# Routed experts by scatter and gather in one stream of slots, beside dense experts in stages

## The chip, the cores and the metric

One core of a Trainium2 chip. Its engines are TensorE (PE), VectorE (DVE), ScalarE (ACT), GpSimd (POOL) and the SyncE queue (SP) that issues most DMAs. They run side by side, each works its instructions in order, and they wait for each other on semaphores. The metric is the device time of one execution in microseconds (us); the median of three runs before is 811.64 us (811.57 to 812.65).

## The reference, cut to what matters

The input x has 8 batches of 512 tokens of 128 features, all fp32. Cut to what matters:

```python
xn = layernorm(x)
# differential attention: 8 heads of 16, two maps of 8 each
scores = einsum('bqhif,bkhif->ibhqk', q, k) * 8 ** -0.5
att = softmax(scores)[0] - diff_weight * softmax(scores)[1]
o = einsum('bhqk,bkhe->bqhe', att, v)
a = (rms_norm(o) * norm_w @ Wo.T + bo) * (1 - diff_weight)
# feed forward: a shared expert and the best 2 of 8 for each token
gates = sigmoid(xn @ Wg); vals, idx = top_k(gates, 2); w = vals / vals.sum()
shared = silu(xn @ Ws1) * (xn @ Ws3) @ Ws2               # 128 -> 256 -> 128
routed = sum over experts of w[e] * (silu(xn @ We1[e]) * (xn @ We3[e]) @ We2[e])
out = x + a + (shared + routed) / 3
```

`w` is zero for six of the eight experts of every token.

## The kernel before, in words

The program goes through the batches in two alternating stages, `attend` and `ffn` (L183 on, `batches`): a hardware loop of three rounds covers two batches each, and what is first and last is written out. The order of each engine's work is written by hand; semaphores with counted values tie the engines.

Attention is computed transposed, keys on partitions. The 16 maps of a batch and four key tiles make 64 tiles of 128 keys by 512 queries. q and k are split into two fp32r parts (`qparts`, `kparts`) and laid by DMAs from SP (`lay_qk`) into operands `qop` and `kop`, in which two maps stand in the two halves of 64 partitions, so that two score matmuls of different halves can stand in the array at once. Two of the 64 rows carry the negated row maximum of a query, so that a score tile comes out with its maximum taken off. For that the maxima must be known first: `score_unit` (L840) computes the scores queries first into the banks `S`, DVE reduces two of them in one instruction of 1024 columns (`row_max`, L624), and after a batch's last one the maxima are split, transposed by PE and laid by four small DMAs (`lay_m`, L247). `score_tile` (L911) puts a tile into one of three banks `ST`, ACT takes its exponential (L474) into `probs`, a ring of 8, and four value matmuls of 32 output rows, in four column groups, add it into the bank `O` (L953). The maxima of batch b+1 are made in the attention stage of batch b: each `score_tile` is followed by a `score_unit` of the other half.

The experts are dense. All nine (eight and the shared one) run over all 512 tokens of a batch, in 18 chunks of 128 hidden features (`ffn`, L983 to L985). Each chunk is two sides of three fp32r matmuls of 512 columns (high times high, high times low, low times high, weights split once at the start and kept in SBUF as `w13h` and `w13l`), Silu on ACT (L505), the product on DVE (L748), a multiplication by the token's gate weight on POOL (L384), and one fp32 matmul down into `O` (L967), three chunks later. The gate weights come from 19 small DVE steps per batch (`top_step`), are transposed, stored to DRAM and broadcast back to all partitions. Between the chunks stand the attention's unpacking (DVE, ST banks), its projection (L1039) and the preparation of batch b+2. ACT loads its function table when it goes from exponentials to Silu and back.

## Time and profile before

| what | value |
|---|---|
| median of 3 runs | 811.64 us |
| profiled execution: time, span | 813.23 us, 811.4 us |
| PE busy | 759.4 us (94%) |
| DVE busy | 589.9 us (73%) |
| ACT busy | 428.3 us (53%) |
| POOL busy | 248.6 us (31%) |
| DMA | 45.40 MB, mean 56 GB/s |
| mean granted PE clock | 0.963 |

The span runs from the first to the last instruction. Busy times are from one profiled execution. Matmuls overlap in the array, so that PE can be shown as busy while it could take more; the starts of successive matmuls show what one costs. An fp32 matmul stands in the trace as two records, an fp32r matmul as one (its type is shown as f32 too). PEld is the loading of weights, which overlaps.

### The profile page before, as it was taken

Reading aid. Unit: us, or ns where it says so; the run is one execution under the profiler, and the core shown is the slowest. Engines: PE = TensorE matmul, PEld = TensorE weight load, DVE = VectorE, ACT = ScalarE, POOL = GpSimd, SP = SyncE. Lnnn points to the kernel's source line nnn. Section 1 sums busy time; section 2 is a strip of 40 time slices with the busy share of each in tenths; the row PEclk is TensorE's granted clock in tenths of the full one; section 3 lists DMA queues with packets and bytes.
Section 4 is the critical chain, followed back from the end, with each engine's and each line's share of the span. In section 5 each row is a group of like instructions: output and inputs, shape, how many; then the busy total and the mean of one; then the engine's idle time right before and its main releaser. Section 6 shows DMA issues by size and latency. Waiting matters only on the chain.

```text
span 811.4 us, 12753 instructions
## 1 busy us (share of the span) xinstructions
PE 759.4 (94%) x3740; PEld 406.7 (50%) x3740; DVE 589.9 (73%) x837; ACT 428.3 (53%) x799; POOL 248.6 (31%) x216
## 2 busy tenths in 40 slices
PE   4367999999999998999999998999999999999997
PEld 4122336743566335753467434663367434653464
DVE  5499998669866896659877696668986597751274
ACT  1101784268733784348832685337853587239722
POOL 5883005420155003440065101550044301530152
PEclk9665899999999999999999999999999999999999
DMA  3562101530052100511023300521015200110010
GB/s 100 133 168 80 29 1 32 130 89 4 2 144 68 40 2 21 143 52 40 2 72 88 91 2 5 135 75 43 1 28 134 72 8 2 56 52 27 1 53 13
DMA packets 36262, 45.40 MB, mean 56 GB/s; under 512 B 3736, under 2 KB 18840, under 8 KB 36184
## 3 DMA queue, kind: packets, MB, share of 16 engines
q1 hardware_dynamic: 30712, 33.70, 15.9%
q10 hardware_dynamic: 4608, 8.39, 3.6%
q0 software_dynamic: 864, 2.36, 1.1%
q8 instruction: 38, 0.62, 0.3%
q14 instruction: 40, 0.33, 0.1%
HBM read 24.78 MB, written 2.23 MB: 33 GB/s over the span
## 4 chain that ended last, share of the span: by engine, by line
PE 88%; DVE 5%; ACT 2%; issue 1%; POOL 1%; DMA 1%; SPq 1%; POOLq 0%; DVEq 0%
PE O L953 17%; PE ST L911 16%; PE O L967 16%; PE S L983 9%; PE S L985 8%; PE S L984 8%; PE S L840 5%; DVE rowmax L624 4%; PE ST L959 2%; PE ST L812 2%; PE ST L803 2%; ACT probs L474 2%; DMA kop<-kparts 1%; PE O L1039 1%; PE O L803 1%
## 5 line engine op out<-in xcount | busy, mean ns | idle before, releaser
L624 DVE TENSOR_REDUCE rowmax<-S 128x2 f32<-128x1024 f32 x256 | 307.8, 1220 | 51.2 <-PE S L840 46.4
L384 POOL TENSOR_TENSOR probs<-probs,rwb 128x512 f32<-128x512 f32 x128 | 169.1, 1323 | 523.8 <-DVE probs L748 523.8
L474 ACT ACTIVATE probs<-ST 128x512 f32<-128x512 f32 x476 | 252.3, 615 | 61.4 <-PE ST L911 58.8
L840 PE MATMUL S<-kop,qop 62*128 62x512 f32 x512 | 208.4, 507 | 26.5 <-DVE rowmax L624 14.3
L911 PE MATMUL ST<-qop,kop 64*128 64x512 f32 x476 | 177.3, 452 | 2.9 <-ACT probs L474 0.2
L748 DVE TENSOR_TENSOR probs<-S,sil 128x512 f32<-128x512 f32 x144 | 98.9, 687 | 99.5 <-PE S L985 99.0
L505 ACT ACTIVATE sil<-S 128x512 f32<-128x512 f32 x144 | 86.2, 599 | 157.9 <-PE S L985 155.2
L911 PEld LDWEIGHTS ST<-qop,kop 64*128 64x128 f32 x476 | 79.4, 187 | 151.4 <-ACT probs L474 124.6
L983 PE MATMUL S<-xh,w13h 128*128 128x512 f32 x288 | 146.5, 509 | 6.3 <-issue 6.3
L967 PE MATMUL O<-probs,w 128*128 128x512 f32 x288 | 148.0, 596 | 0.0
L953 PE MATMUL O<-probs,vop 128*32 128x512 f32 x1024 | 141.1, 608 | 0.4
L985 PE MATMUL S<-xh,w13l 128*128 128x512 f32 x288 | 114.3, 397 | 0.0
L984 PE MATMUL S<-xl,w13h 128*128 128x512 f32 x288 | 113.5, 394 | 0.0
L840 PEld LDWEIGHTS S<-kop,qop 62*128 62x128 f32 x512 | 82.9, 196 | 54.6 <-DVE rowmax L624 40.5
L983 PEld LDWEIGHTS S<-xh,w13h 128*128 128x128 f32 x288 | 54.9, 191 | 34.5 <-issue 23.8
L984 PEld LDWEIGHTS S<-xl,w13h 128*128 128x128 f32 x288 | 55.2, 192 | 21.3 <-issue 14.9
L967 PEld LDWEIGHTS O<-probs,w 128*128 128x128 f32 x288 | 53.1, 188 | 18.1 <-issue 8.0
L985 PEld LDWEIGHTS S<-xh,w13l 128*128 128x128 f32 x288 | 54.6, 190 | 12.9
L953 PEld LDWEIGHTS O<-probs,vop 128*32 128x32 f32 x1024 | 24.4, 108 | 40.4 <-ACT probs L474 25.6
L712 DVE TENSOR_SCALAR o_inv<-o_inv,ndw 128x8 f32<-128x8 f32 x32 | 34.3, 1072 | 0.9
L719 DVE TENSOR_TENSOR o_n<-o_sc 128x128 f32<-128x128 f32 x32 | 24.9, 777 | 0.8
L700 DVE COPY oT<-O 128x512 f32<-128x512 f32 x4 | 2.8, 692 | 28.2 <-PE O L953 28.2
(117 smaller groups left out, 518.0 us busy)
## 6 DMA issues: line engine op xcount, KB each, us to landing
qop<-qparts SPq DMA_DIRECT2D x32, 256.0 KB, 3.6
kop<-kparts SPq DMA_DIRECT2D x32, 256.0 KB, 6.0
rwb<-w_scr SPq DMA_DIRECT2D x32, 256.0 KB, 3.7
rwb<-w_scr ACTq DMA_DIRECT2D x32, 256.0 KB, 3.3
xin<-in_L_attn_x SPq DMA_DIRECT2D x8, 256.0 KB, 3.5
sil<-in_L_ffn_We POOLq DMA_DIRECT2D x16, 128.0 KB, 4.0
res<-in_L_attn_x SPq DMA_DIRECT2D x8, 256.0 KB, 3.2
out_x<-res SPq DMA_DIRECT2D x8, 256.0 KB, 2.3
```

What stands on the lines that cost most here:

```text
L384: nc.gpsimd.tensor_tensor(hid[:, c % NHB, :], hid[:, c % NHB, :], rwb[:, e % NRW, :], ALU.mult).then_inc(s_hw, 1)
L474: nc.scalar.activation(probs[:, s % NP, :], banks[s % len(banks)], ACT.Exp, scale=SCALE).then_inc(s_p, 1)
L505: nc.scalar.activation(sil[:, c % 2, :], S[c % 2][:, 0, :], ACT.Silu).then_inc(s_si, 1)
L624: V.reduce_max(rowmax[:, u // QT * HALVES:(u // QT + 1) * HALVES, u % QT], S[u % 2][:, :, :], AX).then_inc(s_mx, 1)
L748: V.tensor_tensor(hid[:, c % NHB, :], S[c % 2][:, 1, :], sil[:, c % 2, :], ALU.mult)\
L840: ins = mm(S[u % 2][:, h, :], qop[par][at:at + TERMS, c, t * P:(t + 1) * P], kop[par][at:at + TERMS, c, :], start=True, stop=True, tile_po ...
L911: mm(banks[s % len(banks)], kop[par][at:at + ROWS, c, t * P:(t + 1) * P], qop[par][at:at + ROWS, c, :], start=True, stop=True, tile_positi ...
L953: mm(O[VW * j:VW * (j + 1), :], vop[par][:, t, (4 * g + j) // MAPS, :], probs[:, s % NP, :], start=(t == 0), stop=(t == QT - 1), tile_posi ...
L967: mm(O[:, :], w2[:, c // FC, c % FC, :], hid[:, c % NHB, :], start=(c == 0), stop=last).then_inc(s_y, 1)
L983: mm(dst, w13h[:, c // FC, at], xh[par][:, :], start=True, stop=False)
L984: mm(dst, w13h[:, c // FC, at], xl[par][:, :], start=False, stop=False)
L985: mm(dst, w13l[:, c // FC, at], xh[par][:, :], start=False, stop=True).then_inc(s, 1)
```

## The change

The program is rewritten as one list of 146 slots, numbered -12 to 133, that every engine walks through (in the new program all loops are written out; there is no hardware loop). The 128 slots from 0 on have four score tiles each, 16 slots a batch. Slot s also computes four row maxima of slot s+12 (`LEAD`), now one bank of 512 and one DVE instruction each, and the value matmuls of slot s-1. There are two `S` banks, two `ST` banks, `O`, and three banks `F`: F[0] and F[1] for the two up sides, F[2] for down and for all side jobs of attention (`other`: transposes, projections, maxima rows). `claim` makes PE wait until a bank's last reader is done.

At the start all eight batches are normalised, transposed and gated, before the slots. 42 DVE steps (`route`), two per quarter of a slot, find each token's two experts and its two rows in a DRAM buffer `xs`, sorted by expert, each expert padded to a multiple of 256 rows. The buffer is filled with zeros by three DMAs. POOL scatters 32 tiles of 128 tokens twice by indirect DMA (64, three a slot from slot -5 on). 16 tiles of 256 tokens of the shared expert run in every second slot from -10 to 20; 39 tiles of 256 rows of routed tokens in every second slot from 24 to 100. A routed tile's weights (0.39 MB) come from DRAM by an expert number that SP reads from SBUF, asked for three slots ahead, with three buffers. Its rows are transposed on PE, both sides computed in plain fp32, silu(h) written as h * (1 + tanh(h/2)) with the half put into the weights of the sum, and its result is stored to DRAM (`ys`). From slot 103 on POOL gathers both rows of each token by indirect DMA (64, three a slot), and DVE adds them, weighted, to the output rows (`combine`, from slot 112 on). Exponentials and tanh stand mixed on ACT.

Weights are laid out on the host in the new program (transposed projections, the three matrices of an expert side by side); the split into fp32r parts is gone for the experts and stays for q and k. GpSimd also has the unpacking of attention (`unpack`, three operations per four slots). The diff is nearly the whole file; its core:

```diff
-            def ffn(b, par, more, prep):
-                pe.wait_ge(s_p, TILES * (b + 1))
-                pe.wait_ge(s_xs, 2 * b + 2)
-                pe.wait_ge(s_w13, 2 * (E + SHARED))
-                pe.wait_ge(s_wbig, 16 * (1 + FC))
-                pe.wait_ge(s_w2s, 1)
-                for c in range(CH):
-                    if more and c < 2:
-                        pe.wait_ge(s_mx, UNITS * (b + 2) - 1 + c)
-                    if c >= 2:
-                        pe.wait_ge(s_hm, CH * b + c - 1)
-                    for side, s in ((0, s_h1), (1, s_h3)):
-                        at = slice(side * FF + c % FC * P, side * FF + c % FC * P + P)
-                        dst = S[c % 2][:, side, :]
-                        mm(dst, w13h[:, c // FC, at], xh[par][:, :], start=True, stop=False)
-                        mm(dst, w13h[:, c // FC, at], xl[par][:, :], start=False, stop=False)
-                        mm(dst, w13l[:, c // FC, at], xh[par][:, :], start=False, stop=True).then_inc(s, 1)
...
+    TOK = 256
+    SH_TILES = BATCH * SEQ // TOK
+    RT_TILES = BATCH * SEQ * TOPK // TOK + E - 1
+    TILES = SH_TILES + RT_TILES
+    ROWS = RT_TILES * TOK
+    CMAX = BATCH * SEQ // TOK
+    NW = 3
+    POST = 6
+    LEAD = 12
+    SH0 = -10
+    RT0 = SH0 + 2 * SH_TILES + 2
+    GATHER0 = RT0 + 2 * RT_TILES + 1
+    COMBINE0 = SLOTS - 16
+    SCAT0 = -5
...
+            def load_tile(r):
+                if r == 0:
+                    sp.wait_ge(s_rt, R_EXP)
+                e = sp.value_load(jidx[0:1, r:r + 1], min_val=0, max_val=E - 1)
+                if r >= NW:
+                    sp.wait_ge(s_y, SH_TILES + r - NW + 1)
+                sp.dma_start(wrt[r % NW][:, :], wexp[bass.ds(e, 1), :, :].rearrange("e p f -> (e p) f")).then_inc(s_wl[r % NW], 16)
+                if r == 0:
+                    sp.wait_ge(s_sc, 16 * TOPK * NT)
+                if r >= 2:
+                    sp.wait_ge(s_xt, r - 1)
+                sp.dma_start(xst[r % 2][:, :, :], xs[TOK * r:TOK * r + TOK, :].rearrange("(p s) d -> p s d", s=2)).then_inc(s_xl[r % 2], 16)
...
+            def scatter(n):
+                i, k = n // TOPK, n % TOPK
+                if n == 0:
+                    gp.wait_ge(s_fill, 16 * (ROWS // P // 26))
+                    gp.wait_ge(s_rt, R_IDX2)
+                    gp.wait_ge(s_xn, NT)
+                G.indirect_dma_start(xs[:, :], bass.IndirectOffsetOnAxis(ap=slot_i[:, k, i:i + 1], axis=0),
+                                     xn[:, i, :], None).then_inc(s_sc, 16)
+            def gather(n):
+                b, t, k = n // (QT * TOPK), n // TOPK % QT, n % TOPK
+                if n == 0:
+                    for i in range(2):
+                        gp.wait_ge(s_yst[i], 16 * ((RT_TILES + 1 - i) // 2))
+                    gp.wait_ge(s_sc, 16 * TOPK * NT)
+                    gp.wait_ge(s_xT, BATCH)
+                if b == BATCH // 2 and t == 0 and k == 0:
+                    gp.wait_ge(s_v, BATCH)
+                G.indirect_dma_start(gbuf[b][:, k, t, :], None, ys[:, :],
+                                     bass.IndirectOffsetOnAxis(ap=slot_i[:, k, QT * b + t:QT * b + t + 1], axis=0)).then_inc(s_g[b], 16)
...
+            def tanh_half(j):
+                act.wait_ge(s_h1, j + 1)
+                if j >= 2:
+                    act.wait_ge(s_u, j - 1)
+                A(tb[j % 2][:, :, :].rearrange("p c t -> p (c t)"), F[0][:, :], ACT.Tanh, scale=0.5).then_inc(s_th, 1)
...
+                    if 0 <= slot < SLOTS:
+                        exp_tile(slot, k)
+                    if k == 0:
+                        j = tile_at(slot - 2)
+                        if j is not None and j >= SH_TILES:
+                            copy_y(j - SH_TILES)
+                        j = tile_at(slot)
+                        if j is not None and j >= SH_TILES:
+                            copy_xsT(j - SH_TILES)
+                        j = tile_at(slot - 1)
+                        if j is not None:
+                            tanh_half(j)
...
+            def row_max(slot, k):
+                n = 4 * slot + k
+                q, hf = slot % QUADS, slot // 8 % 2
+                dve.wait_ge(s_s, n + 1)
+                if slot % 8 == 0 and k == 0 and slot >= 16:
+                    dve.wait_ge(s_ms, 3 * (slot // 8 - 1))
+                V.reduce_max(rowmax[hf][:, 1 - k % 2, q // 2 % HC, (2 * q + k // 2) % QT:(2 * q + k // 2) % QT + 1],
+                             S[n % 2][:, :], AX).then_inc(s_mx, 1)
...
+            def gate_u(j):
+                dve.wait_ge(s_th, j + 1)
+                if j >= 2:
+                    dve.wait_ge(s_hid, j - 1)
+                V.scalar_tensor_tensor(out=ub[j % 2][:, :, :].rearrange("p c t -> p (c t)"),
+                                       in0=tb[j % 2][:, :, :].rearrange("p c t -> p (c t)"), scalar=1.0, in1=F[0][:, :],
+                                       op0=ALU.add, op1=ALU.mult).then_inc(s_u, 1)
+            def gate_hid(j):
+                dve.wait_ge(s_u, j + 1)
+                dve.wait_ge(s_h3, j + 1)
+                if j >= 2:
+                    dve.wait_ge(s_y, j - 1)
+                V.tensor_tensor(hid[j % 2][:, :, :].rearrange("p c t -> p (c t)"), F[1][:, :],
+                                ub[j % 2][:, :, :].rearrange("p c t -> p (c t)"), ALU.mult).then_inc(s_hid, 1)
...
+                    if slot + LEAD < SLOTS:
+                        row_max(slot + LEAD, k)
+                    for _ in range(2):
+                        if step < R_STEPS:
+                            route(step)
+                            step += 1
+                    n = (slot + LEAD) // 8 - 1
+                    if (slot + LEAD) % 8 == 0 and 0 <= n < 2 * BATCH and k < 3:
+                        max_parts(n, k)
+                    if k == 0:
+                        j = tile_at(slot - 2)
+                        if j is not None and j < SH_TILES:
+                            add_shared(j)
+                    j = tile_at(slot - 1)
+                    if j is not None and k == 1:
+                        gate_u(j)
+                    if j is not None and k == 2:
+                        gate_hid(j)
...
+            def up(j, side):
+                bank = claim(side, (s_u, s_hid)[side], j + 1)
+                if side == 0:
+                    if j == 0:
+                        pe.wait_ge(s_wsh, 16)
+                    if j < SH_TILES:
+                        pe.wait_ge(s_xTc, j // 2 + 1)
+                    else:
+                        r = j - SH_TILES
+                        pe.wait_ge(s_wl[r % NW], 16 * (r // NW + 1))
+                        pe.wait_ge(s_xtc, r + 1)
+                for c in range(FC):
+                    at = side * FF + c * P
+                    last = mm(bank[:, c * TOK:(c + 1) * TOK], weights(j)[:, at:at + P], tokens(j), start=True, stop=True)
+                last.then_inc((s_h1, s_h3)[side], 1)
+            def down(j):
+                if j < SH_TILES:
+                    bank = claim(2, s_ysh, j + 1)
                 else:
-                    pe.wait_ge(s_hw, RCH * b + c + 1)
-                mm(O[:, :], w2[:, c // FC, c % FC, :], hid[:, c % NHB, :], start=(c == 0), stop=last).then_inc(s_y, 1)
-            def ffn(b, par, more, prep):
-                pe.wait_ge(s_p, TILES * (b + 1))
-                pe.wait_ge(s_xs, 2 * b + 2)
-                pe.wait_ge(s_w13, 2 * (E + SHARED))
-                pe.wait_ge(s_wbig, 16 * (1 + FC))
-                pe.wait_ge(s_w2s, 1)
-                for c in range(CH):
-                    if more and c < 2:
-                        pe.wait_ge(s_mx, UNITS * (b + 2) - 1 + c)
-                    if c >= 2:
-                        pe.wait_ge(s_hm, CH * b + c - 1)
-                    for side, s in ((0, s_h1), (1, s_h3)):
-                        at = slice(side * FF + c % FC * P, side * FF + c % FC * P + P)
-                        dst = S[c % 2][:, side, :]
-                        mm(dst, w13h[:, c // FC, at], xh[par][:, :], start=True, stop=False)
-                        mm(dst, w13h[:, c // FC, at], xl[par][:, :], start=False, stop=False)
-                        mm(dst, w13l[:, c // FC, at], xh[par][:, :], start=False, stop=True).then_inc(s, 1)
-                    if c >= LAG:
-                        down(b, c - LAG)
-                    if more and c == 0:
-                        do_rwT(b + 1)
-                    if c == 1:
-                        pe.wait_ge(s_oe, GROUPS * (b + 1))
-                        do_oT(b, 0, 2)
-                    if more and c == 2:
-                        do_mT(b + 2, ST[1])
-                    if c == 3:
-                        if more:
-                            pe.wait_ge(s_rwc, b + 2)
-                        do_oT(b, 1, 0)
-                    if prep:
-                        x = b + 2
-                        if c == 5:
-                            pe.wait_ge(s_mc, b + 3)
-                            do_xT(x, 1)
-                        if c == 6:
-                            pe.wait_ge(s_on, OE_STEPS * b + 4)
-                            project(x, 0, 2, s_q)
-                        if c == 7:
-                            pe.wait_ge(s_on, OE_STEPS * b + 8)
-                            project(x, 1, 0, s_k)
-                        if c == 9:
-                            do_v(x, 1)
-                        if c == 11:
-                            pe.wait_ge(s_vc, x + 1)
-                            do_g(x, 1)
-                    if c == 8:
-                        pe.wait_ge(s_on, OE_STEPS * b + 4)
-                        if prep:
-                            pe.wait_ge(s_qr, b + 3)
-                        do_oT(b, 2, 2)
-                    if c == 10:
-                        pe.wait_ge(s_on, OE_STEPS * b + 8)
-                        if prep:
-                            pe.wait_ge(s_kr, b + 3)
-                        do_oT(b, 3, 0)
-                    if c == 16:
-                        pe.wait_ge(s_on, OE_STEPS * (b + 1))
-                        tiles_T(ST[2][:, :], lambda t: o_n[:, t, :], ident[:, :], s_nT)
-                for c in range(CH - LAG, CH):
-                    if more:
-                        s = c - CH + LAG
-                        if s < 2 and prep:
-                            pe.wait_ge(s_hm, CH * (b + 1) - 1)
-                        if s == 2:
-                            pe.wait_ge(s_nc, b + 1)
-                            pe.wait_ge(s_hm, CH * (b + 1))
-                        start_attend(b + 1, 1 - par, prep, True, s)
-                    if c == CH - 1:
-                        pe.wait_ge(s_nc, b + 1)
-                        mm(O[:, :], woT[:, :], nT[:, :], start=False, stop=False)
-                    down(b, c, last=c == CH - 1)
-            batches(pe, attend, ffn)
-            finish(BATCH - 1)
-_INS = ['L0_attn_x', 'L0_attn_Wq', 'L0_attn_Wk', 'L0_attn_Wv', 'L0_attn_norm_w', 'L0_attn_Wo', 'L0_attn_bo',
-        'L0_attn_diff_weight', 'L0_ffn_Wg', 'L0_ffn_Ws1', 'L0_ffn_Ws3', 'L0_ffn_Ws2', 'L0_ffn_We1', 'L0_ffn_We3',
-        'L0_ffn_We2']
+                    bank = claim(2, s_yc, j - SH_TILES + 1)
+                pe.wait_ge(s_hid, j + 1)
+                for i in range(2):
+                    for c in range(FC):
+                        last = mm(bank[:, i * P:(i + 1) * P], hid[j % 2][:, c, i * P:(i + 1) * P],
+                                  weights(j)[:, 2 * FF + c * P:2 * FF + (c + 1) * P], start=(c == 0), stop=(c == FC - 1))
+                last.then_inc(s_y, 1)
...
+                even = slot % 2 == 0
+                for k in range(4):
+                    if 0 <= slot < SLOTS:
+                        score_exp(slot, k)
+                    if slot + LEAD < SLOTS:
+                        score_max(slot + LEAD, k)
+                    if k == 0:
+                        j = tile_at(slot)
+                        if j is not None and j >= SH_TILES:
+                            do_xsT(j - SH_TILES)
+                        j = tile_at(slot - 1)
+                        if j is not None:
+                            up(j, 1)
+                    if k == 1:
+                        if 1 <= slot <= SLOTS:
+                            weigh(slot - 1)
+                        if not even:
+                            other(slot)
+                    if k == 2 and even:
+                        other(slot)
+                    if k == 3:
+                        if slot == -10:
+                            do_prefix()
+                        j = tile_at(slot)
+                        if j is not None:
+                            up(j, 0)
+                        j = tile_at(slot - 1)
+                        if j is not None:
+                            down(j)
```

## Rows read from the trace of the kernel before

**Rows 1.** The page, part 1: busy us (share of the span) and instructions.

```profile
PE 759.4 (94%) x3740; PEld 406.7 (50%) x3740; DVE 589.9 (73%) x837; ACT 428.3 (53%) x799; POOL 248.6 (31%) x216
```

**Rows 2.** Stages: stretch, length, busy us of each engine, granted clock, DMA.

```profile
123.60:173.80 50.20, 50.20 (x204) 33.08 (x204) 32.62 (x49) 18.54 (x33) 25.56 (x20) 1.00 0.34 86
173.80:215.40 41.60, 41.07 (x256) 16.10 (x255) 39.24 (x53) 35.20 (x68) 0.00 (x0) 1.00 0.07 20
...
731.00:761.40 30.40, 29.67 (x188) 9.27 (x189) 2.77 (x4) 30.30 (x63) 0.00 (x0) 1.00 0.07 19
```

**Rows 3.** Timeline of one expert chunk: start us, us, engine, line.

```profile
795.31 0.79 PE L983 MATMUL S<-xh,w13h 128*128 128x512 f32 x1
...
795.94 0.39 PE L984 MATMUL S<-xl,w13h 128*128 128x512 f32 x1
...
796.17 0.39 PE L985 MATMUL S<-xh,w13l 128*128 128x512 f32 x1
796.17 0.19 PEld L983 LDWEIGHTS S<-xh,w13h 128*128 128x128 f32 x1
...
797.54 0.79 PE L983 MATMUL S<-xh,w13h 128*128 128x512 f32 x1
```

**Rows 4.** Timeline of four tiles of attention.

```profile
97.87 1.06 PE L953 MATMUL O<-probs,vop 128*32 128x512 f32 x8
...
98.30 1.22 DVE L624 TENSOR_REDUCE rowmax<-S 128x2 f32<-128x1024 f32 x1
...
98.87 0.50 PE L911 MATMUL ST<-qop,kop 64*128 64x512 f32 x1
...
98.87 0.49 PE L840 MATMUL S<-kop,qop 62*128 62x512 f32 x1
...
99.41 2.06 ACT L474 ACTIVATE probs<-ST 128x512 f32<-128x512 f32 x4 [0.55 <-PE ST L911]
99.43 0.18 DVE L600 TENSOR_TENSOR tk<-tk,tks 128x32 f32<-128x32 f32 x1
...
100.92 1.22 DVE L624 TENSOR_REDUCE rowmax<-S 128x2 f32<-128x1024 f32 x1
```

**Rows 5.** Timeline: four fp32 matmuls of 128 columns; four transposes.

```profile
19.25 1.05 PE L816 MATMUL ST<-wqkvT,xT 128*128 128x128 f32 x8
...
145.11 0.60 PE L959 MATMUL ST<-ident,oT 128*128 128x128 f32 x4
```

**Rows 6.** VectorE's timeline: reductions back to back; two operations on PSUM.

```profile
66.94 12.52 DVE L624 TENSOR_REDUCE rowmax<-S 128x2 f32<-128x1024 f32 x11
...
141.44 0.69 DVE L748 TENSOR_TENSOR probs<-S,sil 128x512 f32<-128x512 f32 x1 [2.33 <-PE S L985]
142.05 0.68 DVE L570 TENSOR_TENSOR qparts<-ST,qparts 128x512 fp32r<-128x512 f32 x1
```

**Rows 7.** Groups by line: count, busy us, mean ns, idle before.

```profile
L466 ACT ACT_TABLE_LOAD x15 | 19.2, 1283 | 0.3
...
L331 POOL DMA_DIRECT2D sil<-in_L_ffn_We x16 | 9.0, 564 | 1.8 <-POOL w13l L366 1.8
...
L339 POOL TENSOR_TENSOR ln_s<-ln_s,half 128x4 f32<-128x4 f32 x8 | 8.1, 1014 | 11.3 <-DVE ln_s L562 11.3
```

**Rows 8.** Timeline of the start, and one layout of maxima rows.

```profile
19.22 2.57 SPq L212 DMA_DIRECT2D qop<-qparts  x4
...
26.44 3.53 POOL L356 MEMSET qop<- 128x4096 f32 x1
...
33.20 1.22 PE L840 MATMUL S<-kop,qop 62*128 62x512 f32 x4 [12.11 <-DMA kop<-kparts]
...
221.82 2.78 SPq L247 DMA_DIRECT2D qop<-rows  x4
```

**Rows 9.** DMA issues: engine, count, KB each, median us to landing.

```profile
xin<-in_L_attn_x SPq DMA_DIRECT2D x8, 256.0 KB, 3.5
...
w<-in_L_ffn_We SPq DMA_DIRECT2D x2, 512.0 KB, 5.0
```

1484 lines of the change are left out of this document (736 added, 748 removed).

## The prediction

> **What bounds the kernel now.** I read the page's busy shares first [rows 1]: PE is busy 94%, so the time is a sum of PE-paced stages. The table by stage [rows 2] gives them, at the full granted clock (1.00). After the start and the first batch's row maxima, 41.6 us of attention (64 score tiles with the next batch's maxima beside them) and 50.2 us of dense experts with PE busy 50.20 of 50.20 alternate: 8 batches, of which the last has a shorter attention (30.4 us). So some 8 x 50 = 400 us are experts.
>
> Then the timelines. An expert chunk [rows 3] runs from 795.31 to 797.54: 2.23 us, six fp32r matmuls of 512 columns at 0.23 (start to start in the same rows) and one fp32 matmul of 512 at 0.86 (six records in 2.74 are three of them). 144 chunks x 2.23 = 321 us. Of attention, four tiles [rows 4] take 2.62 us, and PE doesn't fill them: the four value matmuls in column groups take 1.00 (97.87 to 98.87); a pair of score matmuls starts side by side in the two row halves at 98.87, and I take 0.25 for a pair (0.23 is one of 512 columns): 2.0 together. VectorE fills them: two reductions of 1024 and two small steps, from 98.30 to 100.92. ScalarE's four exps start 0.49 apart (2.06 for four) and leave 0.55 idle.
>
> **What the change does to the work.** Each token goes to 2 experts of 8 and to the shared one. Dense: 9 x 4096 tokens in three fp32r passes and one fp32. After: 16 shared tiles of 256 tokens and 39 routed ones (32 plus padding), all plain fp32.
> - PE per tile: four matmuls of 256 columns up, at half of 0.86 = 0.43 each: 1.72. Four of 128 down: four such take 1.05 less the 0.17 drain = 0.22 each [rows 5]: 0.88. Two transposes for a routed tile: four take 0.60, so 0.11 each: 0.22. Sum 2.8. 55 tiles are 150 us of PE where 321 were. The rest of PE is as before.
> - VectorE: no longer one reduction of 1024 per pair (1.14 when back to back, eleven in 12.52 [rows 6]), but two of 512. Nearest row: two PSUM operations of 512 start 0.61 apart [rows 6]. So 4 x 0.61 = 2.44 a slot (2.28 before). Two operations of 512 per tile add 1.22 per two slots.
> - ScalarE: 4 x 0.49 = 1.96 a slot, one tanh of 512 and for a routed tile two copies of 256 (about 0.28) per two slots: 0.5 a slot. The exponentials and the tanh stand mixed in one stream; the trace shows that a table load costs 1.28 us [rows 7], and there are 15 in this line because Silu stages alternate with Exp. I take none in the stream. (The Trainium skill, "ScalarE: Activation LUTs", section on table sets, says that exp's set holds tanh as well, one load for both; no run here shows it. If it were otherwise, see the rivals.)
> - GpSimd loses its 128 multiplies by gate weights, all hidden now behind PE, and gains 64 indirect scatters and 64 gathers.
>
> **The pace of a slot pair.** A routed tile spans two slots, so I lay out two.
> Even slot, PE: pair 0.25, transposes 0.22, pair 0.25, value matmuls 1.00, pair 0.25, a side job (transposes or projections of attention, on average 0.4), pair 0.25, up side one 0.86: 3.5 us. ScalarE and VectorE fit in.
> Odd slot: pair 0.25, up side three 0.86, pair 1.36, value matmuls 2.36, side job 2.73, the third pair. Its result is there at 3.1 (0.4 from start to end of such a matmul in a stream [rows 3]). VectorE is in order: third maximum 3.15 to 3.76, only then the product that makes the hidden tile, to 4.45 (0.69 long [rows 6]). The down matmuls at the end of the slot wait for it: 4.5 to 5.4. So PE idles about 1.5 us in each odd slot, although the two other engines have room: a new wait, PE for VectorE, in place of the old 2.62 rhythm.
> Pair 8.8, slot 4.4. From below: PE's own sum, 7.6 a pair, 3.8 a slot. From above: 5.0, if the side jobs and the single PSUM bank F[2] that they share with the down matmuls cost another 0.6 a slot.
> 102 slots of 128 have tiles: 24 with shared ones (no transposes, 4.3) = 103, 78 with routed ones at 4.4 = 343. Sum 446 (388 to 510).
>
> **Before slot 0.** The first maxima began at 33.2 us, held by the q/k layout DMAs, whose issue began at 19.22 and which landed late [rows 8]. After, all eight batches are normalised and transposed first. SP issues loads 4 to 7 behind 16 layout DMAs (0.64 us each, 2.57 for four [rows 8]): about 29 us, landed at 34 (3.5 to land [rows 9]); four 3.5-us memsets of GpSimd [rows 8] lie between the powers (1.01 each [rows 7]) on the way: 43; then the last normalise, transpose, gate and exp: 47 us (40 to 52).
> Then 12 slots of maxima alone, on VectorE: 48 x 0.64 = 31 us (a bank's cycle: matmul 0.50, reduction 0.69, two banks, with handing over). 42 routing steps: some 27 on 256 columns at 0.42 (a chained 512 takes 0.69, a 32-wide 0.18 [rows 4]), one reciprocal at 1.3, the rest 0.2: 16 us. Five shared tiles at 1.6, residues 2, the wait for the prefix matmul 2. Sum 58 (46 to 64). The zero fill of the token buffer, 5.1 MB at the rate of a load of 512 KB that landed in 5.0 us [rows 9], 49 us, lies beside them. Slot 0 at 105 us.
>
> **The end.** From slot 102 no tiles: ten slots at 2.8, four with combining at 3.6, twelve without maxima at 2.6 (the last batch now: 64 exps in 30.4 us with seven banks, 1.9 per four [rows 2]; two banks add the matmul's latency). 73 us, and a tail of 15 through unpacking, projection and store (12 steps in a chain, each 0.4 to 2 us, and 2 to land): 88. Beside it runs the gather chain, which can't start before the last routed tile is stored (6 us in) and is 64 indirect DMAs long. The trace has none. From below: a direct one of 128 rows, 0.56 us [rows 7]. From above: the same and a small SBUF operation for the index column, 1.01 [rows 7]: 1.57. Between: 1.1. 6 + 70 + unpacking between them on GpSimd 14 + landing, combining, store 9 = 99. So the gathers end last by a little: 100 us (85 to 130). The scatters have from slot -5 to slot 21, some 110 us for 70: hidden. Weights: 39 x 0.39 MB asked for three slots (13 us) ahead, where 512 KB land in 5.0 [rows 9]: hidden. The rows of maxima have less room: issue 2.78 for four [rows 8] and 2 to land, against 4.7 from the copy to their reader; I take nothing, up to 1 us x 16 in the range.
>
> **Sum.** 47 + 58 + 446 + 100 = 651 us of span; the profiled execution had 811.4 span in 813.2, and the median is 811.6, so what lies around the span and the profile's own excess about cancel: 650 us.
>
> **Rivals.**
> 1. *VectorE isn't waited for* (the hidden tile is ready in time because side jobs lag less, maxima are shorter than 0.61): PE's 3.8 a slot, start 86, end 88: 388 + 86 + 88 = 562 to about 590. For it: PE is the one with the largest sum. Against: the order on VectorE puts the third maximum before the product.
> 2. *GpSimd's indirect DMAs set both ends* (about 2 us each): gathers 128 + 29 = 157 instead of 100, scatters 128 and 14 of unpacking against 110 to 126, so some 15 us that PE waits at the first routed tile: 720 us. For it: 1.01 us for four columns shows how slow its small operations are. The Trainium skill, "DMA: Bandwidth & Descriptors", section on the anatomy of one DMA on the gpsimd path, gives about 2.0 us fixed per DMA plus its bytes; if they came one after the other, this rival's estimate would be 2.15 us each, near the same time.
> 3. *Slower than before*: the same place, at a price from which it decides. Every microsecond on an indirect DMA costs 64 us at the end and, past 1.7, another 64 at the start. 812 is reached at 2.7 us each: 64 x 2.7 = 173 + 29 against 100, and 173 against 110 to 126, with the routed tiles 60 late. Against it: nearly five times the direct row.
> 4. *Table loads between exp and tanh*: two per tile, 55 x 2.56 = 141 us on ScalarE, which has 8.8 - 5.5 = 3.3 idle a pair, but the tanh lies ahead of the product: about half shows: 720.
>
> **How the numbers follow.** Forecast (600 to 700): 0.60. Rival 1: 0.15. Rival 2: 0.12. Rival 3: 0.05. Rival 4: 0.03. Other mishaps that are still faster (layout rows late, F[2] contended above the bound): 0.05. Range 575 to 725: its low end takes in most of rival 1, its high end rivals 2 and 4. 0.2% is what a measurement of this kernel can tell from no change; none of the cases ends there. Faster 0.94, same 0.01, slower 0.05.
>
> **What would show it.** Right: PE idle once per odd slot just before the down matmuls, put down to VectorE's product; 8.6 to 9.0 us from one routed tile's down to the next; the first exp at 95 to 112 us; ACT_TABLE_LOAD once or twice; no wait of PE for scatters. Wrong: pace at 7.6 (rival 1) or above 10; GpSimd's indirect operations over 1.6 us, or VectorE waiting long for gathered rows; a table load per tile.

## The result, and the profile after

The changed kernel takes 900.72 us (median of 4, 893.18 to 905.35), the kernel before 811.75 on the same chip: a ratio of 1.1085, 95% interval 1.1008 to 1.1161. Forecast were 650 us, range 575 to 725: wrong, in size and in sign. Ratios here are over undisturbed executions only, while medians and single profiles can hold disturbed ones; this matters for two figures below, both of the variant with extra matmuls.

The page after, its busy shares against [rows 1]:

```profile
span 898.8 us, 11022 instructions
PE 715.0 (80%) x3530; PEld 347.5 (39%) x3530; DVE 503.8 (56%) x1039; ACT 405.7 (45%) x799; POOL 213.6 (24%) x274
```

PE lost only 44 us of busy time where the forecast took 171 out (321 down to 150), and its idle time grew from 52 to 184. The busy figure holds the halved clock and the array's changes of shape as work. The stages are more telling, cut where slot 0, slot 24 and slot 102 begin on PE (stretch, length, busy time of each engine, granted clock, DMA; the answer to [rows 2]):

```profile
0.00:49.00 49.00, 29.72 (x140) 24.09 (x140) 22.82 (x97) 20.19 (x43) 32.72 (x40) 0.63 0.54 186
49.00:150.00 101.00, 61.97 (x150) 33.24 (x150) 53.81 (x109) 5.75 (x10) 35.36 (x36) 0.58 0.15 54
150.00:296.20 146.20, 119.16 (x613) 57.66 (x612) 85.50 (x160) 67.00 (x125) 37.94 (x47) 0.90 0.10 33
296.20:737.00 440.80, 387.01 (x2184) 191.57 (x2184) 279.39 (x516) 246.13 (x497) 31.87 (x63) 0.99 0.27 82
737.00:898.80 161.80, 117.14 (x449) 40.92 (x448) 62.24 (x159) 66.59 (x125) 75.69 (x89) 0.64 0.15 41
```

Forecast: slot 0 at 105 (measured 150.0: +45), 103 for 24 slots (+43), 343 for 78 (+98), 100 for the end (+62). That is the whole difference of 248 us; in the forecast every stage but the start (47, about 49 measured) is too short. The clock is at its upper level (2.4 GHz) only in the middle; in the lead (0.58) and at the end (0.64) much of the time is at 1.2 GHz.

The lead, the twelve slots of row maxima before slot 0, shows something that the kernel before never did. Its timeline, 15 us of it (start, length, engine, line; in brackets the idle time before and its releaser):

```profile
116.50 0.79 PE L933 MATMUL S<-kop,qop 62*128 62x512 f32 x1
117.22 1.62 PE L992 MATMUL F<-xT,wsh 128*128 128x256 f32 x4
117.93 0.69 DVE L690 TENSOR_REDUCE rowmax<-S 128x1 f32<-128x512 f32 x1 [2.01 <-PE S L933]
118.78 0.50 PE L933 MATMUL S<-kop,qop 62*128 62x512 f32 x1
...
124.16 0.96 POOL L357 DMA_INDIRECT xs<-xn,slot_i  x1 [0.31 <-issue]
125.42 0.96 POOL L357 DMA_INDIRECT xs<-xn,slot_i  x1 [0.30 <-issue]
...
127.73 0.60 ACT L500 ACTIVATE tb<-F 128x512 f32<-128x512 f32 x1 [29.99 <-remote]
129.83 0.69 DVE L690 TENSOR_REDUCE rowmax<-S 128x1 f32<-128x512 f32 x1 [11.21 <-remote]
130.58 0.79 PE L933 MATMUL S<-kop,qop 62*128 62x512 f32 x1 [11.30 <-DVE rowmax L690]
```

PE and VectorE use the two `S` banks in turn. The reduction that starts at 129.83 is the one of the score matmul of 116.50, which had ended at 117.29: it comes 12.5 us late, where in a run without this (r5_same, below) such a reduction starts 0.04 us after the matmul's end. VectorE, which waits for nothing but its semaphore, goes on only after the row of GpSimd's indirect DMAs ended at 126.38. ScalarE's tanh at 127.73 is late in the same way (its up side, from 114.50, had ended at 116.57), and PE, with both banks full (the matmul of 118.78 ended at 119.28), stands still with them. The profile finds no releaser ("remote"). I call these late signals. Over the run they are 17 waits, 108.2 us of idle time summed over engines; the kernel before has none.

### The profile page after: what moved, and what is told of

Read it like the earlier page. It is cut to its first block, busy times and chain, and to the rows that moved or that the text cites. A ratio compares the mean times of both kernels' runs of the same rounds, so it can differ in the third digit from the quotient of the medians.

```text
span 898.8 us, 11022 instructions
## 1 busy us (share of the span) xinstructions
PE 715.0 (80%) x3530; PEld 347.5 (39%) x3530; DVE 503.8 (56%) x1039; ACT 405.7 (45%) x799; POOL 213.6 (24%) x274
## 4 chain that ended last, share of the span: by engine, by line
PE 68%; issue 12%; DVE 10%; another core or an unknown queue 4%; SPq 2%; ACT 2%; DMA 1%; POOL 1%; DVEq 0%; ACTq 0%
PE ST L947 19%; PE O L961 14%; PE F L992 14%; PE F L1003 7%; DVE hid L721 4%; PE S L933 3%; DVE rowmax L690 2%; PE F L906 2%; PE F L976 2%; PE F L922 1%; SPq L212 1%; PE F L897 1%; PE F L875 1%; PE F L870 1%
## 5 line engine op out<-in xcount | busy, mean ns | idle before, releaser
L690 DVE TENSOR_REDUCE rowmax<-S 128x1 f32<-128x512 f32 x512 | 349.0, 688 | 306.8 <-PE S L933 242.1
L515 ACT ACTIVATE probs<-ST 128x512 f32<-128x512 f32 x512 | 300.6, 599 | 363.8 <-PE ST L947 319.9
L947 PE MATMUL ST<-qop,kop 64*128 64x512 f32 x512 | 241.0, 523 | 38.7 <-ACT probs L515 22.2
L933 PE MATMUL S<-kop,qop 62*128 62x512 f32 x512 | 244.1, 520 | 34.2 <-DVE rowmax L690 30.6
L992 PE MATMUL F<-xsT,wrt 128*128 128x256 f32 x312 | 88.2, 405 | 0.0
L1003 PE MATMUL F<-wrt,hid 128*128 128x128 f32 x312 | 45.1, 288 | 53.8 <-DVE hid L721 44.3
L357 POOL DMA_INDIRECT xs<-xn,slot_i x64 | 61.8, 966 | 51.0 <-issue 50.9
L1003 PEld LDWEIGHTS F<-wrt,hid 128*128 128x128 f32 x312 | 38.6, 194 | 69.9 <-ACT o_all L479 33.5
L992 PEld LDWEIGHTS F<-xsT,wrt 128*128 128x128 f32 x312 | 52.8, 189 | 25.0 <-issue 20.9
L500 ACT ACTIVATE tb<-F 128x512 f32<-128x512 f32 x55 | 32.6, 592 | 54.8 <-remote 30.0
L992 PE MATMUL F<-xT,wsh 128*128 128x256 f32 x128 | 47.1, 503 | 0.0
L721 DVE TENSOR_TENSOR hid<-F,ub 128x512 f32<-128x512 f32 x55 | 37.4, 680 | 0.0
L992 PEld LDWEIGHTS F<-xT,wsh 128*128 128x128 f32 x128 | 28.1, 242 | 13.5 <-issue 10.0
```

What stands on the lines that cost most here:

```text
L357: G.indirect_dma_start(xs[:, :], bass.IndirectOffsetOnAxis(ap=slot_i[:, k, i:i + 1], axis=0), xn[:, i, :], None).then_inc(s_sc, 16)
L500: A(tb[j % 2][:, :, :].rearrange("p c t -> p (c t)"), F[0][:, :], ACT.Tanh, scale=0.5).then_inc(s_th, 1)
L515: A(probs[:, n % NP, :], ST[n % 2][:, :], ACT.Exp, scale=SCALE).then_inc(s_p, 1)
L690: V.reduce_max(rowmax[hf][:, 1 - k % 2, q // 2 % HC, (2 * q + k // 2) % QT:(2 * q + k // 2) % QT + 1], S[n % 2][:, :], AX).then_inc(s_mx, 1)
L721: V.tensor_tensor(hid[j % 2][:, :, :].rearrange("p c t -> p (c t)"), F[1][:, :], ub[j % 2][:, :, :].rearrange("p c t -> p (c t)"), ALU.mul ...
L933: mm(S[n % 2][:, :], qop[b % 2][at:at + TERMS, c, t * P:(t + 1) * P], kop[b % 2][at:at + TERMS, c, :], start=True, stop=True, tile_positio ...
```

## The experiments

Labels: e are variants, r is the changed kernel or a variant once more. Kernels with the same number in the first column ran on one chip; "remote" is the sum of the waits without a known releaser; slots 24 to 102 are the steady stage of 78 slots.

| chip | kernel | us | slot 0 at | slots 24 to 102 | from 102 | remote |
|---|---|---|---|---|---|---|
| 1 | changed kernel | 900.7 | 150.0 | 440.8 | 161.8 | 108.2 |
| 2 | e1_direct | 846.8 | 133.4 | 445.5 | 138.2 | 0 |
| 2 | e2_none | 827.6 | 133.3 | 444.0 | 120.3 | 0 |
| 2 | e3_group | 799.0 | 129.0 | 419.9 | 125.3 | 0 |
| 2 | e4_hid | 803.7 | 131.6 | 415.5 | 131.9 | 0 |
| 3 | r1_same | 898.4 | 152.6 | 440.7 | 154.8 | 70.5 |
| 3 | e5_both | 821.1 | 149.3 | 390.2 | 145.8 | 83.8 |
| 3 | e6_paced | 859.9 | 133.5 | 442.2 | 145.9 | 13.3 |
| 4 | r2_same | 909.6 | 152.6 | 444.1 | 164.6 | 59.1 |
| 4 | r3_group | 869.5 | 152.2 | 417.1 | 155.6 | 68.9 |
| 4 | r4_hid | 866.1 | 149.3 | 419.9 | 155.3 | 87.8 |
| 4 | e7_all | 783.7 | 121.0 | 391.6 | 142.5 | 35.2 |
| 5 | r5_same | 836.8 | 133.6 | 439.5 | 131.2 | 0 |
| 5 | e8_direct | 836.5 | 132.3 | 445.5 | 126.6 | 0 |
| 5 | e10_land | 840.2 | 133.3 | 445.4 | 131.8 | 0 |
| 5 | e9_busy | 763.7 (profile 785.1) | 118.7 | 391.5 | 159.8 | 0 |
| 6 | r6_same | 892.8 | 150.7 | 443.7 | 147.5 | 107.4 |
| 6 | e11_direct | 844.4 | 133.7 | 442.2 | 136.0 | 0 |
| 6 | e12_busy | 811.6 | 124.6 | 391.6 | 162.4 | 32.5 |

The kernel before took 811.8 to 813.2 us on each. (The first row's chip isn't known; it may be one of the others.) The column "us" is a median for the changed kernel, e5_both, e7_all and e9_busy (four executions each) and e12_busy (ten), and one execution for the others; the stages are those of the profiled execution, which for e5_both, e7_all, e9_busy and e12_busy took 823.3, 788.2, 785.1 and 810.7 us.

**e1_direct and e2_none: are the indirect DMAs the price?** Direct DMAs of fixed rows in place of the scatters and gathers, or none at all.

```diff
-                G.indirect_dma_start(xs[:, :], bass.IndirectOffsetOnAxis(ap=slot_i[:, k, i:i + 1], axis=0),
-                                     xn[:, i, :], None).then_inc(s_sc, 16)
+                gp.dma_start(xs[P * n:P * n + P, :], xn[:, i, :]).then_inc(s_sc, 16)
...
```

In e2_none both are skipped, and the waits for them with them:

```diff
-                        if scat < TOPK * NT:
+                        if False:
...
-                        if gath < TOPK * NT:
+                        if False:
```

> The 64 scatters and 64 gathers become direct GpSimd DMAs of the same 128 rows of 512 B to and from fixed rows (so rows go to the wrong experts). Theory A: it is the indirect form (descriptors made from an index column) that holds up the other engines' semaphores while a row of them runs; direct ones take 0.56 us instead of 0.97 + 0.30 and don't do it: the stalls of 6.5 and 11.2 us before slot 0 go, slot 0 comes at about 125 us instead of 150, the end shrinks by some 40 us: 820 to 850 us. Theory B: any row of GpSimd DMAs does it, per descriptor: time 870 to 900 with shorter but as dense stalls. Theory C (instruction fetch of the written-out program makes the stalls): 890 to 905.

> No scatter and no gather at all: the routed tiles compute on the zero-filled buffer, and the combination reads what stands in its buffers. Theories A and B: everything that these DMAs cost goes: slot 0 at 115 to 120 us, slot 24 at 255, slots from 104 on at 2.8 to 3.6 us instead of 5 to 6: 790 to 820 us. Theory C (instruction fetch): the stalls of 5 to 11 us stay, and so does most of the time: over 870. In all of them slots 32 to 96 stay at 5.66 us each.

e1_direct ended in its range (846.8), e2_none above it (827.6); slot 0 came later than expected in both (133 us against 125 and 115 to 120). The theories aren't parted by them: e3_group and e4_hid below, with all their indirect DMAs, had no late signals on this chip either. What e2_none does show is that with no scatter and no gather at all the kernel is still 16 us slower than before (one execution). So the stream of slots alone, with 444 us for 78 of them, makes the change a loss; the DMAs come on top. Its stage from slot 102 shows that gathers aren't the larger part of the end either:

```profile
705.20:825.50 120.30, 90.66 (x449) 34.70 (x448) 61.30 (x159) 65.77 (x125) 13.27 (x25) 0.87 0.07 20
```

120.3 us where the forecast's 88 stood for the same work without gathers; and 18 us more with direct ones (e1_direct: 138.2, at a granted clock of 0.68 against 0.87). On chip 5 the same kernel took 126.6 us for this stage, at 0.82 (e8_direct), so the greater part of the 18 goes with the clock and not with the DMAs.

**e3_group: the array's changes of shape.** PE's order only: two pairs of score matmuls in a row, the tile's work behind the second and the fourth pair instead of behind each.

```diff
-                    if k == 0:
+                    if k == 1:
                         j = tile_at(slot)
                         if j is not None and j >= SH_TILES:
                             do_xsT(j - SH_TILES)
                         j = tile_at(slot - 1)
                         if j is not None:
                             up(j, 1)
-                    if k == 1:
                         if 1 <= slot <= SLOTS:
                             weigh(slot - 1)
...
-                    if k == 2 and even:
-                        other(slot)
                     if k == 3:
+                        if even:
+                            other(slot)
```

> PE's order within a slot: two pairs of score matmuls together, then the tile work and the value matmuls, then the other two pairs, instead of something after each pair. Theory S: after every change between row halves and the whole array the weight load stands exposed (pair 0.43 instead of 0.25, four f32 matmuls of 256 columns 1.07 instead of 0.86); three changes fewer a slot save 0.5 to 0.6 us: slots 32 to 96 at 5.1, total 830 to 850 us. Rival W: the odd slot is set by the wait for the hidden tile alone and what PE saves it waits: only the even slots shorten, 5.45 a slot, 875 us.

**e4_hid: the wait that the forecast named.** VectorE's order only: the product for the down matmuls one maximum earlier.

```diff
-                    if j is not None and k == 2:
+                    if j is not None and k == 1:
                         gate_hid(j)
```

> VectorE makes the hidden tile right after the gated half, before the third row maximum of the slot. Theory W: PE's wait before the down matmuls (1.27 us in the trace) goes, 1.1 to 1.3 us per odd slot, slots 32 to 96 at 5.05, 55 tiles x 1.2 = 66 us: about 835 us. Rival: the third maximum comes later and with it the score matmul that needs its bank, so that PE waits there instead: 5.4 a slot, 870 us.

On chip 2 both were faster than the kernel before, by 1.6 and 1.0% (one execution each), at 5.38 and 5.33 us a slot against 5.63 to 5.71 of the changed kernel and its two DMA variants. Both totals are under what was expected (830 to 850, and 835), yet a slot gained only about half (5.1 and 5.05 expected): the totals came out low on a chip without late signals. But no control of the changed kernel had run there, and their gain (43 to 102 us, by whether one compares with e1_direct or with the first run) was more than the 25 us that 78 slots at 0.3 give. The next three ran with a control.

**r1_same, e5_both, e6_paced.** The changed kernel again; both reorderings; and the changed kernel with GpSimd paced, so that no more than three indirect DMAs follow each other without a wait for the stream:

```diff
+                if slot >= SCAT0 and scat < TOPK * NT:
+                    gp.wait_ge(s_mx, 4 * (slot + LEAD))
+                if slot >= GATHER0 and gath < TOPK * NT:
+                    gp.wait_ge(s_p, 4 * slot)
```

> The changed kernel itself, once more, with its trace. The two runs that keep the rows of indirect DMAs but change only the order of PE or VectorE show none of the 5 to 11 us stalls. If the stalls belong to this program (rows of indirect DMAs meeting its order of work), this run shows them again at the same places, 893 to 905 us. If they belong to the chip or core that the first runs were on, this one ends near 840 us, slot 0 at about 133 us, and the slots 32 to 96 are still 5.66 us each.

> Both orders at once: score pairs two by two on PE and the hidden tile before the third maximum on VectorE. Theories S and W: the two savings are of different kinds (exposed weight loads, a wait), so they add: 0.57 us a slot for the first alone was partly eaten by the wait in odd slots. Slots 32 to 96 at 4.8 us, total 740 to 760 us, faster than the kernel before by 7 to 9%. If PE is limited by something else in between (banks of the exponentials), they add by half only: 5.1 a slot, 775.

> GpSimd issues its indirect DMAs only as the slots go on (three per slot, it waits for that slot's row maximum or exponential), so that no row of them is longer than three; nothing else is changed. Theory A2 (long rows of indirect DMAs hold up the other engines' semaphores): the stalls go as they did with direct DMAs, slot 0 at 133 us, 845 to 855 us. Theory B2 (it is not the length of the row): stalls of some us stay near the scatters and gathers, 880 us or more.

The steady stages add up well: 440.7 to 390.2 us, 5.65 to 5.00 a slot, where the two alone gave 0.27 and 0.32. And pacing alone took the standing still out of the lead: slot 0 at 133.5 where the control had 152.6. But e5_both lost in its lead what it had won: 149.3, where e3 and e4 had 129 and 132. It missed its range by far (740 to 760 expected, 4.8 us a slot), and e6_paced ended above its own (845 to 855 expected, 859.9). Whether late signals belong to a program's order or to the chip was open.

**r2_same, r3_group, r4_hid, e7_all.** The same kernels on one chip, with e7_all the two reorderings and the pacing together.

> The changed kernel once more, unaltered, on the chip of the three runs beside it. It stood still behind rows of indirect DMAs (slot 0 at 150 to 153 us) in the two profiles so far; the variants that did not stand still ran on another chip. Theory A, the standing still belongs to this program's order: again about 895 to 905 us, slot 0 at 150 us, while the two variants below stay at 129 to 132 us. Rival B, it belongs to the chip or the moment: this run and the two variants below show the same of it, all or none (without it about 860 us here).

> The variant with TensorE's score pairs two by two (its tile's work only behind the second and the fourth pair), once more, on the chip of the run before. It took 799.0 us with slot 0 at 129.0 us. Theory A (program order decides): again 799 us within 5. Rival B (chip or moment decides): if the unaltered kernel beside it stands still, this one does too and takes 820 to 845 us, with slot 0 near 148 us.

> The variant with VectorE's product for the down projection moved ahead of one maximum, once more, on the same chip. It took 803.7 us with slot 0 at 131.6 us. Theory A: again 804 us within 5. Rival B: 825 to 850 us with slot 0 near 149 us, if the unaltered kernel beside it stands still.

> Both reorderings (pairs two by two, product ahead) and the paced GpSimd queue (never more than three indirect DMAs without waiting for the stream). Both reorderings alone took 821 us, of which slot 0 came at 149 us and the slots then 5.03 us each. Theory: the pacing takes the 17 us of the lead and some 10 to 20 us of the later stalls away and leaves the slots at 5.03: 775 to 790 us, about 4% under the kernel before, slot 0 at 130 to 134 us. Rival: the stalls come from the number of indirect DMAs and not from rows of them, and it takes 810 to 825 us.

That order decides is refuted, and chip or moment is left: r3_group and r4_hid, unaltered the kernels of 799 and 804 us, took 869.5 and 866.1 here, with late signals of 69 and 88 us where they had none. Their steady stage is nearly the same (417 and 420 against 420 and 416): all but 4 us of the 62 and 70 lie before slot 24 and behind slot 102, where the rows of indirect DMAs are. Repeated executions of a kernel on one chip agree (893 to 905 of the changed kernel, 816 to 823 of e5_both), which speaks for the chip more than for the moment. e7_all takes 783.7 (775 to 790 expected) against 813.2, a ratio of 0.9623 (0.9586 to 0.9660): faster than the kernel before, on a chip with late signals. It has 35.2 us of them itself, none before slot 0. Its stages:

```profile
49.00:121.00 72.00, 52.49 (x153) 29.44 (x152) 53.44 (x109) 5.75 (x10) 18.23 (x18) 0.69 0.13 47
121.00:252.30 131.30, 115.62 (x613) 56.86 (x612) 85.14 (x160) 65.64 (x125) 55.33 (x65) 0.91 0.18 54
252.30:643.90 391.60, 365.17 (x2185) 187.45 (x2186) 274.00 (x516) 239.98 (x497) 32.03 (x64) 0.99 0.31 92
643.90:786.00 142.10, 105.33 (x449) 38.18 (x448) 62.04 (x159) 66.15 (x125) 75.89 (x89) 0.72 0.18 47
```

**r5_same, e8_direct, e10_land, e9_busy.** e10_land makes GpSimd wait, ahead of every third scatter, until all scatters before have landed; e9_busy is e7_all with small matmuls that nobody reads, to hold TensorE's clock.

```diff
+                if n % 3 == 0 and n:
+                    gp.wait_ge(s_sc, 16 * n)
...
+                    if -9 <= slot < 0:
+                        keep_busy(3, ST[1])
+                    if slot >= GATHER0 + 1:
+                        keep_busy(3, F[1])
```

> The changed kernel, unaltered, as the control of the chip that the three runs beside it use. On three chips so far it took 898 to 910 us with slot 0 at 150 to 153 us (it stood still behind rows of indirect DMAs); on the one chip where no variant stood still it has not been seen. Stalling chip: 898 to 910 us. Chip of the other kind: about 850 to 860 us, slot 0 at 133 us.

> The scatters and gathers as direct GpSimd DMAs of fixed rows (same bytes, same number, same place in the queue; the rows moved aren't the routed ones). It took 846.8 us on the chip that showed no standing still. Theory A, indirectness makes the stalls: on a chip where the control takes 898 us or more, this takes 847 to 860 us with slot 0 near 133 us. Rival B, any row of GpSimd DMAs without a pause does it: it takes about the control's time, slot 0 near 150 us. On a chip without stalls the two can't be told apart.

> Ahead of every third scatter GpSimd waits until all scatters before have landed; the gathers are unaltered. Theory A, descriptors that pile up behind the rows hold the other engines' semaphores: with at most three outstanding the lead has no standing still, slot 0 at 131 to 136 us against the control's 150 us, and the total is 15 to 25 us under the control. Rival B, the issuing itself does it, whatever has landed: slot 0 stays near 150 us, with the stalls at the same places.

> The best version so far (783.7 us: pairs two by two, product ahead, paced GpSimd queue) with three extra bf16 matmuls of 128 columns behind each pair in slots -9 to -1 and behind slot 104, into a bank that nobody reads. Theory A, the granted clock of 0.59 to 0.76 there costs time: the fill lifts it to 0.9 or more, and the lead gets 5 to 10 us and the end 5 to 10 us shorter, 765 to 775 us. Rival B, those stretches wait on VectorE's chain and on GpSimd's gathers, and the clock only follows the idleness: no gain, or 2 to 6 us lost to 180 extra matmuls, 782 to 790 us.

This chip has no late signals, so e8_direct and e10_land tell nothing apart here. But the control now gives the changed kernel without them: 836.8 us (850 to 860 expected), with the same instructions and the same row of indirect DMAs from 85 to 126 us:

```profile
49.00:133.60 84.60, 62.39 (x149) 33.52 (x149) 53.53 (x109) 5.75 (x10) 35.19 (x36) 0.58 0.19 64
133.60:264.30 130.70, 114.05 (x613) 55.62 (x612) 85.18 (x159) 66.65 (x125) 37.93 (x47) 0.94 0.12 37
264.30:703.80 439.50, 385.70 (x2186) 190.68 (x2186) 279.47 (x516) 246.15 (x497) 31.89 (x63) 0.99 0.27 82
703.80:835.00 131.20, 100.43 (x449) 37.00 (x448) 61.67 (x159) 65.88 (x125) 74.94 (x89) 0.77 0.19 50
```

Against the first run: 16.4 us less before slot 0, 15.5 in the first 24 slots, 1.3 in the steady stage, 30.6 at the end. So 64 of the 248 us that the forecast missed go with late signals; 184 are there without them. The 64 can hold some clock: at the end 0.64 was granted against 0.77, and e1_direct and e8_direct, one kernel without late signals, differ by 12 us there at 0.68 and 0.82.

e9_busy took 763.7 us, ratio 0.9384 (0.9345 to 0.9423). That is theory A's number within 1.3 us, but theory A isn't shown by it. e7_all did not run on this chip, and the chip has no late signals: from slot 0 to slot 24, where there is no fill, e9_busy's profile is 18 us shorter than e7_all's (113.3 against 131.3), while its lead, with the fill at 0.93, is 2.3 us shorter. At the end the fill failed in the profiled execution (785.1): from 670 to 686.9 us TensorE was busy 15.5 of 16.9 us at the full clock, and then it was granted half the clock for 85.3 us, through all of which it was busy. Only the last 11 us were at the full clock again. The last 72 us of it:

```profile
711.00:783.00 72.00, 66.38 (x315) 28.32 (x307) 10.26 (x40) 23.44 (x41) 18.41 (x24) 0.57 0.12 32
```

**r6_same, e11_direct, e12_busy.** Control, e8_direct's and e9_busy's kernels again.

> The changed kernel, unaltered, as the control of this chip. It has taken 837 us on one chip (slot 0 at 133.6 us, VectorE and ScalarE never still behind the rows of indirect DMAs) and 893 to 910 us on three others (slot 0 at 150 to 153 us). One of the two again: 835 to 850 us, or 893 to 912 us.

> The scatters and gathers as direct GpSimd DMAs of fixed rows once more (the rows moved aren't the routed ones), beside the control. If the control is of the slow kind: theory A, the standing still needs indirect DMAs, 835 to 860 us and slot 0 at 132 to 134 us; rival B, any row of GpSimd DMAs without a pause does it, 893 us or more and slot 0 near 150 us. If the control is of the fast kind, both say 835 to 850 us and nothing is told apart.

> The best version (pairs two by two, product ahead, paced GpSimd queue, extra bf16 matmuls in slots -9 to -1 and behind slot 104), once more on another chip: it took 763.7 us (760.0 to 785.1) against 812.2 us, in a profile whose last 85 us were at half clock. Theory: the pacing makes it insensitive to the chip, so 760 to 775 us here too, whatever the control does. Rival: where the control is of the slow kind it takes 775 to 790 us, like the version without the fill (783.7 us there).

The control is of the late kind (892.8), and direct DMAs in the same places take the late signals away: 844.4, slot 0 at 133.7, no wait without a releaser. These are single executions, but on the chips with late signals all ten runs with indirect DMAs had them. GpSimd's rows differ, though. The direct ones stand back to back, 28 in 15 us, 0.54 each; an indirect one takes 0.97 and a pause of 0.30. Of e11_direct, then of the changed kernel's page:

```profile
84.99 15.06 POOL L357 DMA_DIRECT2D xs<-xn  x28 [32.64 <-issue]
```

```profile
L357 POOL DMA_INDIRECT xs<-xn,slot_i x64 | 61.8, 966 | 51.0 <-issue 50.9
```

So it takes an indirect DMA, or a row of DMAs that lasts some 40 us instead of 15 to 20; these two I didn't part.

e12_busy refutes its theory: 811.6 us (795 to 821) where e9_busy had 763.7, ratio 0.9848 (0.9815 to 0.9882). Late signals are back (32.5 us, where e7_all, paced in the same way, has 35.2), and the fill, where it doesn't lift the clock, is work: in the last slots, at half clock, a slot takes 6.49 us against 4.84 in e7_all, so 12 extra matmuls cost 1.65 us, 0.14 each. In the lead 75.6 us at 0.75 stand against e7_all's 72.0 at 0.69. On the chips with late signals holding the clock this way was no gain: the fastest kernel there is e7_all (783.7, on chip 4 alone). Whether the fill helps without late signals stays open.

## Why the prediction was wrong, step by step

**The pace of a slot pair** is the step that failed: 4.4 us a slot forecast, upper bound 5.0, measured 5.65, which is 98 of the 248 us (and 28 more in the first 24 slots). The terms of the sum that were too small are PE's: a pair of score matmuls at 0.25 and the full-array work beside it. Two slots take 11.3 us, above the 10 that the forecast named as a sign of being wrong. The wait in the odd slot was as forecast; the prices weren't. PE's timeline of an odd slot and the even one behind it, at the full clock:

```profile
575.32 0.50 PE L947 MATMUL ST<-qop,kop 64*128 64x512 f32 x1
575.32 0.50 PE L933 MATMUL S<-kop,qop 62*128 62x512 f32 x1
575.75 1.13 PE L992 MATMUL F<-xsT,wrt 128*128 128x256 f32 x4
576.82 0.50 PE L947 MATMUL ST<-qop,kop 64*128 64x512 f32 x1
...
577.25 1.06 PE L961 MATMUL O<-probs,vop 128*32 128x512 f32 x8
578.24 0.66 PE L906 MATMUL F<-ident,oT 128*128 128x128 f32 x4
578.83 0.50 PE L947 MATMUL ST<-qop,kop 64*128 64x512 f32 x1
...
580.84 1.13 PE L1003 MATMUL F<-wrt,hid 128*128 128x128 f32 x8 [1.27 <-DVE hid L721]
581.90 0.50 PE L947 MATMUL ST<-qop,kop 64*128 64x512 f32 x1
...
582.33 0.44 PE L976 MATMUL F<-ident,xst 128*128 128x128 f32 x2
582.70 0.50 PE L947 MATMUL ST<-qop,kop 64*128 64x512 f32 x1
...
583.13 1.06 PE L961 MATMUL O<-probs,vop 128*32 128x512 f32 x8
584.13 0.50 PE L947 MATMUL ST<-qop,kop 64*128 64x512 f32 x1
...
584.55 1.16 PE L875 MATMUL F<-wqkvT,xT 128*128 128x128 f32 x8
585.64 0.50 PE L947 MATMUL ST<-qop,kop 64*128 64x512 f32 x1
...
586.07 1.13 PE L992 MATMUL F<-xsT,wrt 128*128 128x256 f32 x4
587.13 0.49 PE L947 MATMUL ST<-qop,kop 64*128 64x512 f32 x1
```

- A pair of score matmuls that stands alone between other work costs 0.43 (575.32 to 575.75), not the 0.25 that I took from one fp32r matmul in a stream of its own shape [rows 3, 4]. Of two pairs in a row, as in e5_both's timeline, each costs 0.33, also the one with full-array work behind it:

```profile
576.15 0.49 PE L947 MATMUL ST<-qop,kop 64*128 64x512 f32 x1
...
576.48 0.39 PE L947 MATMUL ST<-qop,kop 64*128 64x512 f32 x1
...
576.81 1.13 PE L992 MATMUL F<-xsT,wrt 128*128 128x256 f32 x4
```

- The work that follows pays too: an up side 1.07 for 0.86, the transposes of a routed tile 0.37 for 0.22, the down matmuls 1.06 for 0.88. A side job is 0.53 to 1.09, 0.51 a slot on average, where I took 0.4. The value matmuls are 1.00, as forecast.
- Over the steady stage, two slots add up like this (PE, from start to start of successive pieces, us):

| piece | forecast | measured |
|---|---|---|
| 8 pairs of score matmuls | 2.0 | 3.28 |
| 2 up sides | 1.72 | 2.12 |
| value matmuls | 2.0 | 2.04 |
| down matmuls | 0.88 | 1.08 |
| transposes of a routed tile | 0.22 | 0.38 |
| side jobs | 0.8 | 1.02 |
| PE idle | 1.2 | 1.40 |
| two slots | 8.8 | 11.3 |

The prices were there to read. In the kernel before, close to [rows 4], a pair with the value matmuls (column groups, at 97.87) behind it takes 0.43 from 97.44; the first pair behind them takes 0.34, from 98.87 to 99.21; and only inside a stream of its own shape does the next score matmul start 0.23 later:

```profile
97.44 0.50 PE L911 MATMUL ST<-qop,kop 64*128 64x512 f32 x1
...
99.21 0.40 PE L911 MATMUL ST<-qop,kop 64*128 64x512 f32 x1
...
99.44 0.40 PE L911 MATMUL ST<-qop,kop 64*128 64x512 f32 x1
```

So one step into a shape costs about 0.1 us and one out of it another 0.1. In the kernel before there are two such changes in four tiles of attention and none within a chunk of experts; the change puts seven or eight into each slot of 5 us. e3_group changes only the order of PE's pieces: its waits in the steady stage stay the same to 0.1 us (54.8 in all), its pairs fall from 3.28 to 2.83 us in two slots, and it gains 0.27 a slot. That shows the price of a change on the pairs. The excess of the full-array pieces was hardly moved by it (2.12 to 2.06 for the up sides), so that it is the same price is read from their rows and not shown by a variant. The Trainium skill, "TensorEngine Tiling (Array Packing)", section "Key Properties", says that changing the tiling mode, not only the tile, drains TensorE. The trace agrees: 0.43 for a pair alone against 0.33 for one of two. This rule spoke against the change, and I hadn't weighed it.

**The wait for VectorE's product** is as forecast: the text says "about 1.5 us in each odd slot", its own terms give 1.2 (8.8 less 7.6), and 1.27 is seen above. The waits of PE in the steady stage, first of the changed kernel, then of e5_both, where it is gone and the bank shared with the side jobs is the next:

```profile
PE F L1003 <- DVE hid L721: 44.3, 35, 1.3
PE F L1003 <- DVE qparts L587: 9.5, 4, 2.4
```

```profile
PE F L1003 <- ACT o_all L479: 14.7, 20, 0.7
PE F L1003 <- DVE qparts L587: 7.1, 4, 1.8
PE F L1003 <- ACT nT L488: 4.6, 5, 0.9
```

Without it the slot is 5.00 us (e5_both): rival 1 in its mechanism, but at 5.0 a slot instead of 3.8. The waits fall from 53.8 to 26.4 us, and e4_hid, which makes this change alone, gains 25 in the stage.

**Before slot 0.** The start is right (47 forecast, about 49). The lead isn't: 58 forecast, 84.6 without late signals. I summed VectorE's work, and its size was right (53.5 us busy), but it isn't what bounds. PE works 62.4 of the 84.6 us, most of it at 1.2 GHz, and with two banks PE and VectorE alternate: the reductions wait for a matmul that stands behind 2 us of a tile. Of r5_same's timeline:

```profile
104.01 2.04 PE L1003 MATMUL F<-wsh,hid 128*128 128x128 f32 x8 [1.09 <-DVE hid L721]
...
109.31 2.07 PE L992 MATMUL F<-xT,wsh 128*128 128x256 f32 x4
...
112.03 2.07 PE L992 MATMUL F<-xT,wsh 128*128 128x256 f32 x4
...
114.86 0.69 DVE L690 TENSOR_REDUCE rowmax<-S 128x1 f32<-128x512 f32 x1 [2.04 <-PE S L933]
```

From the down matmuls of one tile to the next are 13.5 us; forecast for two slots 9.7. The clock is the smaller part: the kernel with direct DMAs took 83.3 us here at 0.74 (e8_direct) and 84.4 at 0.58 (e1_direct). The order of the two engines counts for more: with both reorderings and pacing the lead is 72.0 us at 0.69 (e7_all), 12.6 less. The 14 us that are left to the forecast's 58 I can't place.

**Slots 0 to 24.** 103 forecast, 130.7 without late signals. The pieces are the same and the clock is 0.94, so the same prices would do it; no run parts them here.

**The end.** 100 forecast, "the gathers end last by a little". Without gathers and at 0.87 it takes 120.3 (the slots 122 to 126 are 3.1 to 4.2 us each, where 2.6 were forecast from [rows 2]); with gathers and without late signals 131.2 at 0.77, where the same slots are at half clock and take 4.6 to 6.1 us; with late signals 148 to 165 for the unaltered kernel.

**GpSimd's indirect DMAs** cost 1.26 us each (0.97 and 0.30), forecast 1.1, rival 2 about 2, rival 3 needed 2.7. So rivals 2 and 3 named the right instruction and the wrong harm: it isn't GpSimd's own time that counts. The Trainium skill, "DMA: Bandwidth & Descriptors", section on the anatomy of one DMA on the gpsimd path, has about 2.0 us fixed per DMA; the issues here stand 1.26 apart and don't wait for each other (r5_same's gathers land 2.6 us after their issue), so the estimate of 2.15 did not hold as a pace.

**Rival 4** fell: the page after has one table load (1283 ns) for 512 exps and 55 tanhs mixed. The Trainium skill's statement that one set holds both ("ScalarE: Activation LUTs", section on table sets) agrees with it.

**What no case held.** Late signals: 64 us in the first run. But even without them the kernel is at 837, slower than before and above my range. With the measured pace in place of mine the two stages with tiles would have been 126 us longer and the forecast about 775: 37 under the time before instead of 162. The rest of the way to 837 is the lead and the end.

**Late signals: what is shown and what isn't.** Shown: the changed kernel has them in four runs of five with a profile and is 56 to 73 us slower there; whether a kernel has them goes by the chip or the moment (r3_group and r4_hid in both); they vanish with direct DMAs where the control has them (e11_direct, one execution) and shrink with rows of three (e6_paced: 70.5 us down to 13.3; but e7_all and e12_busy, paced too, keep 35.2 and 32.5). Open: what in the chip delays the semaphores; whether it is indirectness or the length of the row; and whether outstanding descriptors count, since e10_land ran where nothing was late.

## What to carry to other kernels

Count how often PE changes between row halves, column groups and the full array, and price each piece of work from a row in which its neighbour has another shape (0.43 for a pair stood in the timeline from which I took 0.25); removing half of the experts' matmul time gains nothing if what is left is interleaved piece by piece. Keep pieces of one shape together, put a product that PE waits for ahead of work nobody waits for, and break long rows of GpSimd's indirect DMAs with a wait. Compare a variant with its control on the same chip: here the same kernel took 837 us on one and 893 to 910 in four runs elsewhere.

## What the runs showed of the hardware

- VectorE went on up to 18 us (e5_both, a reduction at 126.68) and ScalarE up to 11 us (the tanh at 127.73 in the first run) after the PE matmul that they waited for had ended, while GpSimd issued rows of indirect DMAs: in all ten runs with such DMAs on chips 1, 3, 4 and 6 of the list, in none of five on chips 2 and 5; the kernel before, on the same chips, moved by under 0.2%.
- Half clock for 85.3 us with TensorE busy throughout (e9_busy's profile), so keeping it busy didn't bring the clock back; three other executions of that kernel took 760 to 767 us.
- A change of shape costs about 0.1 us on each side of a pair of score matmuls (0.43 alone, 0.33 for each of two, 0.23 inside a stream); full-array pieces between pairs take 0.15 to 0.2 us more than in a stream of their own (an up side 1.07 for 0.86).
